# One program for the state-space and the feed-forward stage: first chunk's input made ahead, second matrix's first piece split in four

## The chip, the cores and the metric

The kernel runs on one core of one Trainium2 chip. The metric is the device time of one execution in microseconds, as the median of several runs. Engines by the profile's names: PE is TensorE, PEld its weight loads, DVE is VectorE, ACT is ScalarE, POOL is GpSimd, SP is SyncE, whose queue issues nearly all transfers here.

## The reference

Input x is (2, 2048, 512) float32, the condition t is (2, 512). Two layers follow one another; everything is float32.

```python
# layer 0
mod = t @ Wm + bm                                   # six vectors of 512 per batch element
y_mod = ln(x) * (1 + scale_a) + shift_a
y = x + gate_a * s5(y_mod)                          # diagonal complex recurrence, 128 states
y_norm = ln(y) * (1 + scale_c) + shift_c            # scale_c, shift_c from t @ Wc + bc
h = gelu((y_norm * (1 + scale_ff) + shift_ff) @ W1 + b1)   # 512 -> 2048
z = y + gate_ff * (h @ W2 + b2)                     # 2048 -> 512
# layer 1: conditioned layer norm, attention with 16 heads over 2048 positions,
# projection, second conditioned layer norm, residual
```

## The kernel before

Six stages follow one another: preparation (the condition's vectors, the recurrence's tables), state space, feed-forward, the projection to queries, keys and values, attention, and the last projection. Each is a block of its own with one instruction stream for each engine; engines inside a block meet through semaphores only, and at the end of a block all of them meet at a barrier. Before its end, the state-space block's SP stream also waits for all its loads and for the stores of y (L461).

Every float32 product is made of three matmuls (L36 to L38): an operand is split into a rounded high part and the rest, `hi` and `lo`.

**Preparation** loads Wm (512 x 3072) by three transfers of 2 MB into one tile `wm` (L144); PE's first group of projections waits for the first two of them, the second group for the third and for Wc. ACT copies the projections out, POOL adds the biases (L171), and DVE builds the tables and then the vectors (L366 to L386).

**State space** goes in eight steps c over chunks of 512 positions (c % 2 is the batch element). For each: DVE takes moments of the chunk (`moments`, L578), ACT normalises it into `norm` (L530), PE transposes it (`turn`, L472), ACT applies gain and shift and makes `u` and `u_hi` (`modulate`, L538, L541), POOL makes `u_lo` (L677), PE multiplies into the states (`project_in`), DVE and POOL rotate, scan and rotate back (L641, L664, L645, L650, L672), ACT makes `s_hi` (L548), POOL makes `s_lo` (L682), PE multiplies back (`project_out`, four parts t of 128 positions), and DVE adds the rows (L604). The order of an engine is written out by hand, with chunk c + 1 prepared beside chunk c. SP loads and stores the chunks, and loads three of the four column pieces of W1 (the first two and the last) and, at the last step, `y_first`, the stored first chunk of the result.

**Feed-forward** goes through the same eight chunks. W1 is four pieces (1, 0) to (1, 3), W2 four pieces (2, 0) to (2, 3), each 128 x 2048 values, all kept in `hi` and `lo` parts. For chunk 0 the moments and the normalisation (DVE, L55 to L81, L964), the transposes (PE, L835), gain and shift (ACT, L905) and the split (DVE, L971, L973) come first, among them the split of the first weights: ACT makes the high part of (1, 0), (1, 1), (1, 3), (2, 0) (L893), DVE the low part of (1, 0), (1, 1), (2, 0) (L770), POOL the rest (L1029, L770):

```python
    HI_ACT = [(1, 0), (1, 1), (1, 3), (2, 0)]
    LO_DVE = [(1, 0), (1, 1), (2, 0)]
    POOL = [(1, 3), (2, 1), (1, 2), (2, 2), (2, 3)]
    HELD = [[(1, 0), (2, 0), (1, 2), (2, 2), (2, 3)], [(1, 1), (2, 1)], [(1, 3)]]
    LOADS = [(2, 0), (2, 1), (1, 2), (2, 2), (2, 3)]
```

`HELD` names the three staging tiles (`raw_weight` and two `w_stage`) and what each holds in turn; a load into a tile waits until the piece in it is split. Then each chunk goes through 16 steps j: `up(j)` (12 matmuls into h), ACT's gelu (L911) and high part `h_hi` (L918), DVE's low part `h_lo` (L983), and `down(j)` (12 matmuls into four accumulators). PE's order is up(0), up(1), down(0), up(2), down(1), and so on. up(j) needs piece (1, j // 4), down(j) needs piece (2, j // 4) and h_lo(j). Of chunk 0, PE reads a piece for the first time at up(0), down(0), up(4), down(4), up(8), down(8), up(12), down(12). POOL adds `lift` to the chunk's rows (L1019) and, at the end of a chunk, the result (L1023).

Of the kernel before, what the change touches and what calls it, by code (L numbers as in the profile page):

```python
# [88 lines left out]
def prep_stage(nc, sb, sem, psum, a, ident, columns, s5, x, wgb, vec_dram):  # L89


    wm = sb("wm", [P, KT, 6 * D])
# [38 lines left out]
    with nc.Block() as block:  # L131
        @block.sync
        def _(sp):
# [8 lines left out]
            for n in range(3):  # L142
                cols = slice(2 * n * D, 2 * (n + 1) * D)
                sp.dma_start(wm[:, :, cols], a["L0_cond_Wm"].rearrange("(k p) n -> p k n", p=P)[:, :, cols]).then_inc(ld_wm[n], 16)  # L144
# [29 lines left out]
        def _(pe):  # L174
# [15 lines left out]
            for group, first in enumerate(range(0, 10, SIDE)):  # L190
                if group == 0:
                    pe.wait_ge(ld_wm[0], 16)
                    pe.wait_ge(ld_wm[1], 16)
                if group == 1:
                    pe.wait_ge(bbar_ready, 1)
                    for part in range(2):
                        for k in range(KT):
                            mm = pe.transpose(psum[:, 2 + part, k * P:(k + 1) * P], b_bar[:, part, k * P:(k + 1) * P], ident[:, :])
                        mm.then_inc(bc_tp, 1)
                    pe.wait_ge(ld_wm[2], 16)  # L200
                    pe.wait_ge(ld_wc, 16)
# [14 lines left out]
                for k in range(KT):  # L216
                    for n in range(first, min(first + SIDE, 10)):
                        w = wm[:, k, n * D:(n + 1) * D] if n < 6 else (
                            wc[:, k, (n - 6) * D:(n - 5) * D] if n < 8 else wm[:, k, (n - 8) * D:(n - 7) * D])
# [11 lines left out]
        def _(act):  # L231
# [19 lines left out]
            for j in range(2 * KT):  # L251
                act.wait_ge(gb_tp, j + 1)
                act.activation(wm[:, j % KT, j // KT * D:(j // KT + 1) * D], psum[:, j % 4, :], ACT.Copy).then_inc(gb_ready, 1)
# [135 lines left out]
def s5_stage(nc, sb, sem, psum, a, ident, columns, s5, x, w1_stage, y_first, vec_dram, y_dram):  # L389
# [4 lines left out]
    y = [sb(f"y{b}", [P, TT, D]) for b in range(B)]  # L394
    norm = sb("norm", [P, TT, D])
# [7 lines left out]
    u_hi, u_lo = ([sb(f"u_{part}{n}", [P, KT, CH], F32R) for n in range(NU)] for part in ("hi", "lo"))  # L403
# [5 lines left out]
    x_ld, y_ld, y_st = ([sem(f"s5_{n}{b}") for b in range(B)] for n in ("x_ld", "y_ld", "y_st"))  # L409
    gate_ld, w1_ld, y_first_ld, start = sem("s5_gate_ld"), sem("s5_w1_ld"), sem("s5_y_first_ld"), sem("s5_start")  # L410
# [9 lines left out]

    def rows(dram, c):
# [4 lines left out]
    with nc.Block() as block:  # L426
        @block.sync
        def _(sp):
            def load_x(c):
                sp.wait_ge(norm_ready, TT * (c - 1))  # L430
                sp.dma_start(x[c % B][:, :, :], rows(a["x"], c)).then_inc(x_ld[c % B], 16)

            def load_y(c):
                if c >= B:
                    sp.wait_ge(y_st[c % B], 16 * (c // B))
                sp.dma_start(y[c % B][:, :, :], rows(a["x"], c)).then_inc(y_ld[c % B], 16)

            def store(c):
                sp.wait_ge(y_ready, TT * (c + 1))
                sp.dma_start(rows(y_dram, c), y[c % B][:, :, :]).then_inc(y_st[c % B], 16)  # L440

            for b in range(B):
                sp.dma_start(gate[b][:, :], vec_dram[V_GATE_A, b:b + 1, :].broadcast_to((P, D))).then_inc(gate_ld, 16)
            load_x(2)
            load_y(0)
            for tile, piece in zip(w1_stage, (0, 1, 3)):
                sp.dma_start(tile[:, :, :], a["L0_cond_W1"].rearrange("(k p) f -> p k f", p=P)[:, :, piece * D:(piece + 1) * D]).then_inc(w1_ld, 16)
            for c in range(STEPS):
                if c + 3 < STEPS:
                    load_x(c + 3)  # L450
                if c > 0:
                    load_y(c)
                if c == STEPS - 1:
                    sp.dma_start(y_first[:, :, :], rows(y_dram, 0)).then_inc(y_first_ld, 16)
                if c > 0:
                    store(c - 1)
            store(STEPS - 1)
            sp.wait_ge(w1_ld, 48)
            sp.wait_ge(y_first_ld, 16)
            for b in range(B):  # L460
                sp.wait_ge(y_st[b], 16 * NCH)  # L461

        @block.tensor
        def _(pe):
            def turn(c, ks):

                pe.wait_ge(norm_ready, TT * (c + 1))
                for k in ks:
                    if KT * c + k >= 2:
                        pe.wait_ge(u_ready, 2 * (KT * c + k - 1))  # L470
                    for t in range(TT):
                        mm = pe.transpose(psum[:, TR + k % 2, t * P:(t + 1) * P], norm[:, t, k * P:(k + 1) * P], ident[:, :])  # L472
                    mm.then_inc(tr_ready, 1)

            def project_in(c):

                if c >= B:
                    pe.wait_ge(back_ready, 4 * (c - 1))
                for k in range(KT):
                    pe.wait_ge(ulo_ready, KT * c + k + 1)  # L480
                    for n in range(2):
# [38 lines left out]
        def _(act):  # L520
# [38 lines left out]
            for c in range(STEPS):  # L559
                if c + 2 < STEPS:  # L560
                    take_root(c + 2)
                if c + 1 < STEPS:
                    modulate(c + 1)
# [1548 lines left out]
```

## Time and profile before

| | us |
|---|---|
| median of 3 runs | 3102.53 (3099.68 to 3111.16) |
| the profiled execution | 3103.81 |
| its span, from the first to the last instruction | 3102.0 |
| PE busy in the span | 2956.4 (95%) |
| mean granted TensorE clock | 0.977 |

An instruction belongs to a line of the kernel. "Idle before" is how long its engine had nothing to do ahead of it, and the releaser is what ended that. Names in a row are those of the tiles without their numbers (`w_hi` for both matrices' high parts, `w_stage` for the two staging tiles, which also carry g and a chunk of y in the feed-forward stage).

### The profile page before, as it was taken

What the parts mean: (1) busy time and instruction counts of PE and PEld (TensorE: products, weight loads), DVE (VectorE), ACT (ScalarE), POOL (GpSimd) and SP (SyncE); (2) the same over time, 40 slices, a digit from 0 to 9 for tenths busy, and PEclk for the clock granted to TensorE, in tenths of its full rate; (3) what the DMA queues carried; (4) which work ended last, traced back from release to release, by engine and by line L of the source; (5) the groups of instructions that cost most, each with busy time, mean ns of one, the idle gap of its engine ahead of it and who ended that gap; (6) DMA issues with size and microseconds to landing.
All of it is one profiled execution on the core that took longest, in us unless ns stands there. A gap on an engine that the chain in (4) does not pass through costs nothing. (4 is left out here: it accounts for less than half of the span.)

```text
span 3102.0 us, 41235 instructions
## 1 busy us (share of the span) xinstructions
PE 2956.4 (95%) x15050; PEld 1937.7 (62%) x15050; DVE 2013.7 (65%) x3567; ACT 1509.9 (49%) x2743; POOL 1741.9 (56%) x742
## 2 busy tenths in 40 slices
PE   4897999999999799999999999999999999999987
PEld 2786878878887687765555555555555555555456
DVE  7864332222221555778888888888888888888448
ACT  3532233232332222146666666666666666666634
POOL 2763210111110211138888888888889888888834
PEclk7998999999999899999999999999999999999989
DMA  5433100000000446375668866687765877666557
GB/s 220 154 136 122 41 22 7 28 28 27 28 14 4 166 181 216 132 186 118 133 129 186 185 133 136 130 185 158 153 137 128 172 163 163 135 132 129 109 198 276
DMA packets 148124, 395.73 MB, mean 128 GB/s; under 512 B 11430, under 2 KB 29354, under 8 KB 127448
## 3 DMA queue, kind: packets, MB, share of 16 engines
q0 software_dynamic: 22608, 164.64, 26.5%
q1 hardware_dynamic: 125322, 228.50, 23.7%
q8 instruction: 122, 2.00, 0.3%
q14 instruction: 72, 0.59, 0.1%
HBM read 144.25 MB, written 83.92 MB: 74 GB/s over the span
## 5 line engine op out<-in xcount | busy, mean ns | idle before, releaser
L1679 ACT ACTIVATE probs<-psum 128x512 f32<-128x512 f32 x2048 | 1053.2, 612 | 551.2 <-PE psum L1597 548.5
L1705 DVE TENSOR_REDUCE part_max<-psum 128x1 f32<-128x512 f32 x1984 | 1219.0, 681 | 123.0 <-PE psum L1582 120.4
L1812 POOL TENSOR_TENSOR pair<-probs 128x2048 f32<-128x2048 f32 x255 | 1194.2, 4714 | 150.5 <-ACT probs L1679 144.9
L1597 PE MATMUL psum<-queries,keys 97*128 97x512 f32 x2048 | 849.7, 417 | 5.2 <-ACT probs L1679 2.8
L1582 PE MATMUL psum<-keys,queries 96*128 96x512 f32 x1984 | 802.5, 405 | 2.8
L1597 PEld LDWEIGHTS psum<-queries,keys 97*128 97x128 f32 x2048 | 386.5, 189 | 341.2 <-issue 210.9
L1609 PE MATMUL psum<-probs,values 128*32 128x512 f32 x4096 | 494.0, 600 | 0.0
L1582 PEld LDWEIGHTS psum<-keys,queries 96*128 96x128 f32 x1984 | 376.8, 190 | 125.5 <-DVE part_max L1705 48.4
L983 DVE TENSOR_TENSOR h_lo<-w_stage,h_hi 128x512 fp32r<-128x512 f32 x128 | 99.5, 777 | 515.8 <-ACT h_hi L918 515.8
L911 ACT ACTIVATE w_stage<-psum,b_col 128x512 f32<-128x512 f32 x128 | 88.1, 689 | 498.2 <-PE psum L38 498.2
L1609 PEld LDWEIGHTS psum<-probs,values 128*32 128x32 f32 x4096 | 107.0, 109 | 234.4 <-ACT probs L1679 136.1
L36 PE MATMUL psum<-ffn_u_hi,w_hi 128*128 128x512 f32 x512 | 203.0, 396 | 3.2 <-DVE b_col L1000 3.1
L36 PE MATMUL psum<-w_hi,h_hi 128*128 128x512 f32 x512 | 204.2, 399 | 1.0 <-DVE h_lo L983 1.0
L37 PE MATMUL psum<-w_hi,h_lo 128*128 128x512 f32 x512 | 202.9, 396 | 0.0
L38 PE MATMUL psum<-ffn_u_lo,w_hi 128*128 128x512 f32 x512 | 202.6, 396 | 0.0
L37 PE MATMUL psum<-ffn_u_hi,w_lo 128*128 128x512 f32 x512 | 202.5, 395 | 0.0
L38 PE MATMUL psum<-w_lo,h_hi 128*128 128x512 f32 x512 | 202.2, 395 | 0.0
L1023 POOL TENSOR_TENSOR w_stage<-w_stage 128x512 f32<-128x512 f32 x16 | 20.1, 1284 | 320.1 <-DVE w_stage L989 320.1
L1795 POOL DMA_DIRECT2D pair<-pair x157 | 136.1, 867 | 105.6 <-issue 51.5
L1023 POOL TENSOR_TENSOR y_first<-w_stage,y_first 128x512 f32<-128x512 f32 x16 | 20.2, 1292 | 287.1 <-DVE w_stage L989 287.1
L1268 ACT ACTIVATE qk_hi<-psum,bqkv_col 128x512 fp32r<-128x512 f32 x64 | 44.0, 687 | 213.0 <-PE psum L38 206.6
L1729 DVE TENSOR_TENSOR summed<-psum,summed 128x512 f32<-128x512 f32 x65 | 45.0, 692 | 125.4 <-PE psum L1629 125.4
(312 smaller groups left out, 3733.6 us busy)
## 6 DMA issues: line engine op xcount, KB each, us to landing
pair<-pair POOLq DMA_DIRECT2D x157, 1024.0 KB, 7.3
queries<-q_parts SPq DMA_DIRECT2D x96, 256.0 KB, 5.2
keys<-k_parts SPq DMA_DIRECT2D x42, 512.0 KB, 8.9
x<-in_x_dram SPq DMA_DIRECT2D x8, 1024.0 KB, 7.8
y<-in_x_dram SPq DMA_DIRECT2D x8, 1024.0 KB, 6.1
y_rows<-y SPq DMA_DIRECT2D x8, 1024.0 KB, 4.4
qkv_z<-z_rows SPq DMA_DIRECT2D x8, 1024.0 KB, 5.6
q_parts<-qk_hi SPq DMA_DIRECT2D x32, 256.0 KB, 2.0
```

What stands on the lines that cost most here:

```text
L36: nc.tensor.matmul(out, w_hi, x_hi, start=first, stop=False)
L37: nc.tensor.matmul(out, w_lo, x_hi, start=False, stop=False)
L38: return nc.tensor.matmul(out, w_hi, x_lo, start=False, stop=last)
L911: act.activation(g[j % 2], psum[:, H + j % 2, :], ACT.Gelu_apprx_tanh, bias=b1_col[:, j:j + 1]).then_inc(g_ready, 1)
L983: dve.tensor_tensor(h_lo[j % NH][:, :], g[j % 2], h_hi[j % NH][:, :].bitcast(F32), ALU.subtract).then_inc(glo_ready, 1)
L1582: nc.tensor.matmul(ring_slot(), queries[count % NQ][0:R, h, qt * P:(qt + 1) * P], keys[b][0:R, h, kc * CH:(kc + 1) * CH], start=True, stop ...
L1597: nc.tensor.matmul(psum[:, SC + unit % 3, :], keys[place(count)[0]][0:R + 1, h, kt * P:(kt + 1) * P], queries[count % NQ][0:R + 1, h, :], ...
L1609: mm = nc.tensor.matmul(psum[h * HD:(h + 1) * HD, OUT, :], values[b][:, kt, h * HD:(h + 1) * HD], probs[tile % NPROB][:, h, :], start=(kt ...
L1679: act.activation(probs[tile % NPROB][:, h, :], psum[:, SC + unit % 3, :], ACT.Exp).then_inc(exp_ready, 1)
L1705: dve.tensor_reduce(part_max[:, h * TT + qt, kc:kc + 1], max_slot(), AX.X, ALU.max).then_inc(max_read, 1)
L1795: pool.dma_start(pair[number % NPAIR][:, :, :], pair[(number - 1) % NPAIR][:, :, :], accum_op=ALU.add).then_inc(folded[n % 2], 16)
L1812: pool.tensor_tensor(pair[number % NPAIR][:, :, :], probs[2 * number % NPROB][:, :, :], probs[(2 * number + 1) % NPROB][:, :, :], ALU.add) ...
```

## The change

The two stages become one block: each engine runs its state-space stream and then its feed-forward stream, with no barrier between. What follows is moved with it.

- The feed-forward input of chunk 0 is made by the state-space stage as a ninth chunk, c = 8, beside steps 6 and 7: moments and inverse on DVE, normalisation and modulation on ACT, transposes on PE, the low part on POOL. `y_first` is loaded at step 3 instead of step 7, and b1's rows are loaded at the start.
- (1, 0) is split in the state-space stage: ACT makes the high part after step 6, DVE the low part at the start of step 7. SP then loads (2, 0) into its place at step 7.
- The feed-forward streams of ACT, DVE, POOL and SP begin with `finished`, which waits until the last rows are added; PE's begins with a wait for the ninth chunk's u_lo. Counters that chunk 0 would have raised are raised by hand.
- (2, 0) is split in four parts of 512 columns, ACT and DVE following each other. All six other pieces go to POOL, in the order in which PE needs them, after DVE's last part. The product of b2 and the gate (`lift`) moves from DVE to POOL.
- W1 and W2 parts become tiles of one piece each. Some tiles are lent to the preparation, for which Wm is loaded in six transfers of 1 MB instead of three of 2 MB.

```diff
 # preparation
-            for n in range(3):
-                cols = slice(2 * n * D, 2 * (n + 1) * D)
-                sp.dma_start(wm[:, :, cols], ...[:, :, cols]).then_inc(ld_wm[n], 16)
+            for n in range(6):
+                sp.dma_start(wm[n][:, :, :], ...[:, :, n * D:(n + 1) * D]).then_inc(ld_wm[n // 2], 16)
 # state space, SP
+        sp.dma_start(ahead["b1_rows"][:, :], ...).then_inc(small_ld, 16)
-            for tile, piece in zip(w1_stage, (0, 1, 3)):
+        for piece, tile in enumerate(w1_stage[:2]):
...
-                if c == STEPS - 1:
+            if c == B + 1:
                 sp.dma_start(y_first[:, :, :], rows(y_dram, 0)).then_inc(y_first_ld, 16)
+            if c == STEPS - 1:
+                sp.wait_ge(wlo_dve, 1)
+                sp.dma_start(w1_stage[0][:, :, :], ...W2 piece 0...).then_inc(w_ld[0], 16)
             if c > 0:
                 store(c - 1)
         store(STEPS - 1)
-            sp.wait_ge(w1_ld, 48)
-            sp.wait_ge(y_first_ld, 16)
-            for b in range(B):
-                sp.wait_ge(y_st[b], 16 * NCH)
 # PE: turn(c + 1, ...) without "if c + 1 < STEPS"; ACT: take_root, normalise up to c + 2 <= STEPS
             modulate(c + 1)
...
             split_state(c)
+            if c == STEPS - 2:
+                act.wait_ge(norm_ready, TT * STEPS)
+                act.wait_ge(w1_ld, 32)
+                act.activation(ahead["w1_hi"][:, :, :], w1_stage[0][:, :, :], ACT.Copy).then_inc(whi_ready, 1)
 # DVE
-                if c + 2 < STEPS:
+            if c + 2 <= STEPS:
                 moments(c + 2)
                 invert(c + 2)
+            else:
+                dve.wait_ge(whi_ready, 1)
+                dve.tensor_tensor(ahead["w1_lo"][:, :, :], w1_stage[0][:, :, :], ahead["w1_hi"][:, :, :].bitcast(F32), ALU.subtract).then_inc(wlo_dve, 1)
+    def finished(engine):
+        engine.wait_ge(cy_ready, TT * STEPS)
+        engine.wait_ge(y_ready, TT * STEPS)
+        engine.wait_ge(shi_ready, 2 * STEPS)
+        engine.wait_ge(slo_ready, 2 * STEPS)
+    def first_input(engine):
+        engine.wait_ge(ulo_ready, KT * (STEPS + 1))
 # feed-forward
+    HI_ACT = [(1, 0), (2, 0)]
+    LO_DVE = [(1, 0), (2, 0)]
+    POOL = [(1, 1), (1, 2), (2, 1), (2, 2), (1, 3), (2, 3)]
+    HELD = [[(1, 0), (2, 0), (1, 2), (2, 2), (1, 3), (2, 3)], [(1, 1), (2, 1)]]
+    LOADS = [(1, 2), (2, 1), (2, 2), (1, 3), (2, 3)]
...
 # ACT, after finished and six sem_inc
+            for f in range(FP):
+                act.activation(w2_hi[p][:, f, :], raw(w, p)[:, f, :], ACT.Copy).then_inc(whi_ready, 1)
 # DVE, after finished, six sem_inc and the copy of b1_col
+            for f in range(FP):
+                dve.wait_ge(whi_ready, 1 + f + 1)
+                dve.tensor_tensor(w2_lo[p][:, f, :], raw(w, p)[:, f, :], w2_hi[p][:, f, :].bitcast(F32), ALU.subtract).then_inc(wlo_dve, 1)
 # POOL
+        state_space["finished"](pool)
+        pool.wait_ge(wlo_dve, 1 + FP)
+        for n, (w, p) in enumerate(POOL):
+            wait_loaded(pool, w, p)
+            if w == 2 and p >= NP - B:
+                state_space["stored"](pool, p - (NP - B))
+            pool.tensor_copy(part(w1_hi, w2_hi, w, p), raw(w, p)).then_inc(whi_pool, 1)
+            pool.wait_ge(whi_pool, n + 1)
+            split_low(pool, w, p, wlo_pool)
 # one block
+                def _(pe):
+                    one["tensor"](pe)
+                    two["tensor"](pe)
```

## Rows read from the trace of the kernel before

**Rows 1.** The page: PE's busy tenths, the span in 40 slices of 77.55 us.

```profile
PE   4897999999999799999999999999999999999987
```

**Rows 2.** Windows: us, busy us (count) by engine, granted clock, DMA share, GB/s.

```profile
13.00:15.00 2.00, 0.00 (x0) 0.00 (x0) 1.71 (x9) 0.00 (x0) 0.00 (x0) 1.00 1.02 420
82.00:84.00 2.00, 0.00 (x0) 0.00 (x0) 2.00 (x4) 0.00 (x0) 0.00 (x0) 0.98 1.04 384
...
155.60:174.60 19.00, 18.54 (x114) 16.18 (x113) 14.94 (x29) 9.75 (x15) 14.41 (x11) 1.00 0.49 167
191.70:210.60 18.90, 18.43 (x114) 16.10 (x114) 11.24 (x14) 7.44 (x11) 14.35 (x11) 1.00 0.31 112
244.50:272.50 28.00, 9.12 (x31) 7.04 (x32) 21.49 (x33) 12.17 (x11) 4.71 (x1) 0.63 0.45 131
```

**Rows 3.** Timeline of PE across the boundary: start, us, engine, line, [idle before].

```profile
243.20 0.27 PE L38 MATMUL psum<-s_d_lo,u_hi 128*128 128x128 f32 x1
...
267.60 0.49 PE L36 MATMUL psum<-ffn_u_hi,w_hi 128*128 128x512 f32 x1 [3.09 <-DVE b_col L1000]
274.83 0.39 PE L36 MATMUL psum<-w_hi,h_hi 128*128 128x512 f32 x1
280.42 0.39 PE L36 MATMUL psum<-w_hi,h_hi 128*128 128x512 f32 x1
```

**Rows 4.** Timeline of DVE and ACT: boundary, split of constants, preparation.

```profile
206.51 0.77 ACT L541 ACTIVATE u_hi<-psum,columns 128x512 fp32r<-128x512 f32 x1
243.51 0.69 DVE L604 TENSOR_TENSOR y<-psum,y 128x512 f32<-128x512 f32 x1 [2.05 <-PE psum L38]
249.37 1.91 ACT L893 ACTIVATE w_hi<-raw_weight 128x2048 fp32r<-128x2048 f32 x1 [21.54 <-PEq L426]
260.42 2.28 DVE L770 TENSOR_TENSOR w_lo<-raw_weight,w_hi 128x2048 fp32r<-128x2048 f32 x1
75.58 2.18 ACT L557 ACTIVATE s_c_hi<-prod 128x512 fp32r<-128x512 f32 x4
79.94 2.49 DVE L624 TENSOR_TENSOR s_c_lo<-prod,s_c_hi 128x512 fp32r<-128x512 f32 x4
269.84 1.28 ACT L911 ACT_TABLE_LOAD   x1
31.68 1.29 DVE L356 TENSOR_TENSOR s_b_lo<-psum,s_b_hi 128x512 fp32r<-128x512 f32 x2 [5.35 <-ACT s_b_hi L248]
```

**Rows 5.** Timeline of PE and POOL in steps 6 and 7 of the state space.

```profile
226.41 0.50 PE L36 MATMUL psum<-s_c_hi,s_hi 128*128 128x512 f32 x1 [1.36 <-DVE y L604]
230.87 0.73 PE L36 MATMUL psum<-s_c_hi,s_hi 128*128 128x512 f32 x1
...
198.88 2.52 POOL L664 TENSOR_TENSOR turned<-prod 128x512 f32<-128x512 f32 x2 [4.22 <-DVE prod L641]
211.03 2.54 POOL L682 TENSOR_TENSOR s_lo<-state,s_hi 128x512 fp32r<-128x512 f32 x2
217.84 2.53 POOL L664 TENSOR_TENSOR turned<-prod 128x512 f32<-128x512 f32 x2 [4.27 <-DVE prod L641]
```

**Rows 6.** Timeline of ACT, DVE and POOL in chunk 0 of the feed-forward stage.

```profile
272.24 0.69 ACT L911 ACTIVATE w_stage<-psum,b_col 128x512 f32<-128x512 f32 x1 [1.12 <-PE psum L38]
273.71 0.69 DVE L983 TENSOR_TENSOR h_lo<-w_stage,h_hi 128x512 fp32r<-128x512 f32 x1 [0.37 <-ACT h_hi L918]
310.08 2.84 DVE L983 TENSOR_TENSOR h_lo<-w_stage,h_hi 128x512 fp32r<-128x512 f32 x1 [4.92 <-ACT h_hi L918]
305.77 1.90 POOL L1029 CAST w_hi<-raw_weight 128x2048 fp32r<-128x2048 f32 x1 [5.36 <-DMA raw_weight<-in_L_cond_W_dram]
307.75 4.62 POOL L770 TENSOR_TENSOR w_lo<-raw_weight,w_hi 128x2048 fp32r<-128x2048 f32 x1
```

**Rows 7.** DMA issues from 0 to 345 us: KB each, median us to landing.

```profile
raw_weight<-in_L_cond_W_dram SPq DMA_DIRECT2D x5, 1024.0 KB, 5.2
w_stage<-in_L_cond_W_dram SPq DMA_DIRECT2D x3, 1024.0 KB, 12.8
```

More of the change, by code:

```diff
@@ L402, in s5_stage @@
     u = [sb(f"u{n}", [P, CH]) for n in range(2)]
-    u_hi, u_lo = ([sb(f"u_{part}{n}", [P, KT, CH], F32R) for n in range(NU)] for part in ("hi", "lo"))
+    u_hi, u_lo = ([sb(f"u_{part}{n}", [P, KT, CH], F32R) for n in range(NU - 1)] + [ahead[f"u_{part}"]] for part in ("hi", "lo"))
     prod = sb("prod", [P, 4, CH])
@@ L419, in s5_stage, with chunk_in @@
     TR, BU, CY = 0, 2, 6
+    def chunk_in(c):
+        return x[c % B] if c < STEPS else y_first
     def rows(dram, c):
@@ L701, in ffn_stage @@
+def ffn_stage(nc, sb, sem, psum, a, ident, columns, state_space, ahead, stage, y_first, vec_dram, y_dram, z_dram):
+    NP = 4
+    FP = FT // NP
+    w1_hi, w1_lo = ([ahead[f"w1_{n}"]] + [sb(f"w1_{n}{p}", [P, KT, FP * P], F32R) for p in range(1, NP)] for n in ("hi", "lo"))
+    w2_hi = [sb(f"w2_hi{p}", [P, FP, D], F32R) for p in range(NP - B)] + ahead["w2_hi"]
+    w2_lo = [sb(f"w2_lo{p}", [P, FP, D], F32R) for p in range(NP)]
     y = [y_first, stage[1]]
-    norm = sb("ffn_norm", [P, TT, D])
+    norm = ahead["norm"]
@@ L2054, in cond_seq_kernel @@
         with ExitStack() as weights:
-            w1_stage = [raw_weight] + [scope(weights)(f"w1_stage{n}", [P, KT, D]) for n in (1, 2)]
-            y_first = scope(weights)("y_first", [P, TT, D])
+            keep = scope(weights)
+            w1_stage = [raw_weight] + [keep(f"w1_stage{n}", [P, KT, D]) for n in (1, 2)]
+            y_first = keep("y_first", [P, TT, D])
+            with ExitStack() as early:
+                plain = scope(early)
+                x = [plain(f"s5_x{n}", [P, TT, D]) for n in range(B)]
+                lent = [plain(f"lent{n}", [P, KT, D]) for n in range(2)]
+                y = [plain(f"s5_y{n}", [P, TT, D]) for n in range(B)]
+            ahead = {f"w1_{part}": keep(f"w1_{part}0", [P, KT, D], F32R) for part in ("hi", "lo")}
+            ahead.update({f"u_{part}": keep(f"u_{part}_first", [P, KT, CH], F32R) for part in ("hi", "lo")})
+            ahead["w2_hi"] = [keep(f"w2_hi_late{b}", [P, KT, D], F32R) for b in range(B)]
+            ahead["norm"], ahead["b1_rows"] = keep("norm", [P, TT, D]), keep("b1_rows", [FT, P])
+            ahead["y"] = y
+            lent = [tile[:, :, :] for tile in y + [ahead["norm"]] + lent]
             with ExitStack() as state_space:
```

951 lines of the change are left out of this document (471 added, 480 removed).

## The prediction

> **What bounds the kernel now.** I read the page first. PE is at nine tenths in nearly every slice; the first two, the fourth, the fourteenth and the last two are lower [rows 1]. The fourth slice is the boundary that the change touches, so I went to the windows, then to each engine's timeline across it. The window of 28 us there has PE busy for 9.12 us at a granted clock of 0.63 [rows 2]. PE's timeline shows the hole: its last state-space matmul starts at 243.20 (ends 243.47), its first feed-forward matmul at 267.60, and `down(0)` at 274.83, 5.59 us before `down(1)` [rows 3]. Between them lie the last row addition (ends 244.20), the store and the barrier up to 249.37 [rows 4], then chunk 0's moments, normalisation, transposes and split. From `down(0)` on PE runs step after step of 5.59 us (2.80 for an `up`, 2.80 for a `down`). So the price of the change is how much earlier `down(0)` comes, and whether what PE needs later still comes in time. All times below are in the time of before; a shift of the preparation is added at the end.
>
> **Change part by part.**
>
> *Wm in six transfers.* PE's first projections wait for 4.19 MB of Wm, and DVE idles 5.35 us behind them before s_b_lo [rows 4], so this is on the path of the preparation. The present transfers run at 420 GB/s; transfers with rows of 2 KB (the chunks of x, the pieces of W1) ran at 384 [rows 2]. 4.19 MB take 10.0 us at 420 and 10.9 at 384. Bounds 0 and 0.9 us; I take 0.7 later, near the upper end, since the row length is like that of the 384. Three more issues on SP come ahead of transfers that are needed later.
>
> *The ninth chunk on DVE and ACT in step 6: nothing.* The window from 155.60, one step long, holds the same work for an earlier chunk: 19.00 us with DVE busy 14.94. Step 6, without it, takes 18.90 with DVE at 11.24 [rows 2]. The 3.7 us are covered by PE's 18.4 busy us. Then the split of (1, 0): ACT's modulation ends at 207.3, the normalisation and s_hi are six copies of that kind, about 4 us, w1_hi takes 1.91 and w1_lo on DVE 2.28 [rows 4]: it ends near 215.5. DVE has nothing else then until step 7's products, which start about 1.3 us before POOL's 217.84 [rows 5]. If that cover were gone, step 7's products would be late by the excess. y_first is loaded four steps early; its SP issue costs 0.5 us ahead of a store that waits anyway.
>
> *PE in step 7.* The ninth chunk adds 16 transposes, 2.1 us at full clock. PE idles now because DVE's additions come late (1.36 us before 226.41) [rows 5], and they fit in there. But POOL now makes two u_lo before s_lo. In step 6, which has them, s_lo starts 211.03 - 198.88 = 12.15 us after the first `turned` [rows 5]. Step 7's `turned` starts at 217.84, so s_lo starts at 229.99 and its halves are done at about 231.3 and 232.5, while PE is free at 229.3. `project_out(7)` therefore begins 2.0 us later than PE could, with a second stop of 0.55, where it now begins at 230.87 [rows 5]. On the other side, the part from 226.41 took 4.46 us [rows 5] where the last ones, at full clock, come every 0.69 + 2.05 = 2.74 [rows 4]: after PE's idle time the granted clock was at its lower level, 1.2 GHz. If it stays at 2.4 GHz the state space ends 0.7 us earlier than now, if it falls as long as before 2.5 later. I take no change: last matmul ends 243.5, last addition 244.2.
>
> *The boundary.* Barrier and store go (the stores drain behind POOL's late pieces); b1's transpose is one matmul. Each engine waits and raises six counters: between 0.2 us (one releaser, as from PE to DVE) and 1.0; the whole boundary of before, from the last addition to ACT's first copy, took 5.2 us with all of it. I take 0.4: `up(0)` and ACT's first part of (2, 0) start at 244.6. Now the order from there. PE: `up(0)` to 247.4, `up(1)` to 250.2. ACT: four 128x512 copies take 2.18 us [rows 4], to 246.8; the table load 1.28 [rows 4], to 248.1; then gelu and h_hi to h_lo's start 1.47 (272.24 to 273.71) [rows 6], so h_lo(0) starts at 249.6 and ends at 250.3. `down(0)` starts at 250.4, instead of 274.83: **24.4 us earlier**. DVE's four parts take 2.49 [rows 4] behind ACT's first, so they end at 247.8, and `down(0)` does not wait for them.
>
> *POOL's six pieces.* A piece takes 1.90 + 0.08 for the cast and 4.62 for the low part [rows 6]; I use 6.9 (the longest low part of before was 5.04). A load lands after 5.2 us at the median [rows 7]. POOL starts at 247.9. (1,1) is done at 254.8, needed by `up(4)` at 264.4. (1,2), loaded from 247.8, is done at 261.7, needed at 286.8. (2,1), loaded from 254.8, is done at 268.6, needed by `down(4)` at 250.4 + 4 x 5.59 = 272.8. (2,2) 275.5 for 295.1; (1,3), whose load waits for (2,2), 275.5 + 5.2 + 6.9 = 287.6 for 309.1; (2,3) 299.7 for 317.5. The smallest slack is 4.2 us. `lift` (1.3 on DVE) and L1019 come after and end before 310, where they began at 312.
>
> *POOL against DVE.* The row that matters is h_lo at 310.08: 2.84 us long instead of 0.69, and it ends at 312.92, 0.55 after POOL's low part ends at 312.37 [rows 6]. So h_lo waits out a POOL subtraction that is under way. From its start to the `down` that needs it there are 5.6 - 1.65 = 3.95 us, so a collision costs PE something only if h_lo comes within 1.3 us of the start of a 4.65 us low part, at most 1.3 us each. There are six now, where only POOL's five were. By the order above, the low part of (1,2) starts at 257.3 and h_lo(2) comes at 257.7: about 0.9 lost. Bounds 0 and 3 us; I take 1.0.
> The Trainium skill has the rule (SBUF — State Buffer, "Who interferes with whom"): a VectorE instruction with two SBUF inputs and a GpSimd instruction that reads SBUF exclude each other for a whole instruction, and the one that issues first wins. The trace agrees, with the 2.84 us. By it a collision is decided by hundredths of a microsecond, which is the first rival.
>
> **The sum.** 24.4 earlier, less 0.7 (Wm), less 1.0 (collisions): 22.7. The profiled execution took 3103.81 (1.8 around its span), which gives 3081.1; it stood 1.3 above the median of the runs. On the median: 3102.5 - 22.7 = **3080**. Later stages are the same instructions.
>
> **Rivals.**
>
> *1. POOL's first low part gets ahead of h_lo(0).* POOL's cast starts at 247.9, so its first low part wants to start at 249.8; h_lo(0) wants 249.6. The margin is 0.2 us, made of terms that I know to 0.1 each. If POOL is first, h_lo(0) ends 0.55 after it: 249.8 + 4.7 + 0.55 = 255.0, and `down(0)` at 255.1, 4.7 us later; with PE idle for that long the clock may fall, as after 226.41 [rows 5], another 0 to 2 us. Gain 16 to 18: **3085 to 3087**. For it: the thin margin; against: ACT, at 246.8, has a head start on DVE.
>
> *2. PE's clock is low in the first `up`s.* PE is idle for 1.1 to 1.5 us after the last state-space matmul. Before, 1.36 us of idle time was followed by 1.7 us lost in the next part [rows 5], but no fall came at once after 243.47. If it falls, or if the state-space tail ends 2.5 later, `up(0)` takes up to 5.6, h_lo(0) falls behind POOL's low part and rival 1 comes too. Gain 13 to 15: **3087.5 to 3089.5**.
>
> *3. The other side: loads of the pieces come late.* (1,2), (2,2), (1,3) and (2,3) pass through one tile, each load waiting for the split before it, so the last is ready at 247.6 + 4 (L + 7) with a landing time L. Needed at 317.5, it costs nothing up to L = 10.5. The three loads into `w_stage` had a median of 12.8 [rows 7], under the traffic of step 0: then 326.8, **3089**, no real change against rival 1. It ends slower than 3118 only when it costs 38 us, from L = 20. For it: stores and y loads share the queue. Against: the loads into `raw_weight`, at this very place, 5.2.
>
> *4. The parts hide nothing.* If chunk 8's work delayed steps 6 and 7 by all it adds (3.7 on DVE, 4.2 for the weights, 2.1 on PE), 10 us of the gain would go: 3090. The window of a full step speaks against it [rows 2].
>
> **How the numbers follow.** My forecast 0.52, with 3076 to 3084 as its own range (Wm 0 to 0.9, collisions 0 to 3, tail -0.7 to +0.7, wake-up 0.2 to 1.0). Rival 1: 0.23. Rival 2: 0.10. Rivals 3 and 4 with some gain left: 0.09; slower: 0.03. Better than 3075: 0.03. The range of 3075 to 3088 leaves out the 0.03 below, half of rival 2, and rivals 3 and 4: 0.2. A difference of 0.5%, 15.5 us, is about what a measurement of this kernel can tell from no change, so the border is 3087.0: faster 0.52 + 0.03 + 0.22 + 0.02 = 0.79, within it 0.18, slower 0.03.
>
> **What would show it.** Right: PE's gap between its last state-space and first feed-forward matmul is about 1.2 us instead of 24.1, `down(0)` 7 us after it; PE's wait before `project_out(7)` is about 2 us, for POOL's s_lo; steps 2 to 6 stay near 18.95; POOL's pieces end near 300. Rival 1: h_lo(0) is over 4 us long. Rival 2: the granted clock is half in the window of `up(0)`. Wm: the last vector L386 comes 0.7 later. Wrong would be a wait of PE for a POOL piece, or step 7 starting late behind w1_lo.

## The result and the profile after

The kernel after runs in 3078.85 us (median of 4 runs, 3076.78 to 3080.23), the kernel before in 3102.2 beside it: ratio 0.9919, 95% interval 0.9898 to 0.994. The profiled execution took 3080.23 with a span of 3078.4, against 3102.0 before: 23.6 us less.

The page of after, PE's busy tenths in 40 slices of 76.96 us, answers to [rows 1]: the fourth slice is full now.

```profile
PE   4899999999998999999999999999999999999987
```

The timeline of PE in after, from the last step of the state space to the last `down` (start, duration, [idle before <- what ended it]); it answers to [rows 3] and [rows 5].

```profile
227.43 0.50 PE L36 MATMUL psum<-s_c_hi,s_hi 128*128 128x512 f32 x1 [0.48 <-DVE s_y L604]
232.03 0.73 PE L36 MATMUL psum<-s_c_hi,s_hi 128*128 128x512 f32 x1 [1.65 <-POOL s_lo L684]
...
245.93 0.49 PE L36 MATMUL psum<-u_hi_first,w_hi 128*128 128x512 f32 x1 [1.03 <-DVEq L966]
246.26 0.39 PE L37 MATMUL psum<-u_hi_first,w_lo 128*128 128x512 f32 x1
...
251.82 0.49 PE L36 MATMUL psum<-w_hi,h_hi 128*128 128x512 f32 x1
...
313.63 0.51 PE L36 MATMUL psum<-w_hi_late,h_hi 128*128 128x512 f32 x1 [3.55 <-DVE h_lo L1002]
...
345.16 0.40 PE L36 MATMUL psum<-u_hi_first,w_hi 128*128 128x512 f32 x1
...
978.28 0.40 PE L38 MATMUL psum<-w_lo,h_hi 128*128 128x512 f32 x1
```

The same two places in before, `up(0)` of chunk 1 and the last matmul of the stage:

```profile
360.91 0.39 PE L36 MATMUL psum<-ffn_u_hi,w_hi 128*128 128x512 f32 x1
...
1002.42 0.40 PE L38 MATMUL psum<-w_lo,h_hi 128*128 128x512 f32 x1
```

`down(0)` stands at 251.82 instead of 274.83, 23.0 us earlier; the last matmul of the stage stood at 1002.42 before and stands at 978.28, 24.1 earlier. Between these two rows lie two changes that nearly cancel. From `down(0)` to `up(0)` of chunk 1, chunk 0 takes 345.16 - 251.82 = 93.34 us, where before it took 360.91 - 274.83 = 86.08: **7.3 us lost**. From there to the last `down`, 978.28 - 345.16 = 633.12 instead of 1002.42 - 360.91 = 641.51: **8.4 us gained**, in chunks whose instructions the change leaves alone. The stages behind took 0.6 us longer in this execution, so 23.6 are left in the whole.

Where chunk 0 loses them, in the timeline of DVE and POOL in after (answers to [rows 6]):

```profile
250.91 0.78 DVE L1002 TENSOR_TENSOR h_lo<-w_stage,h_hi 128x512 fp32r<-128x512 f32 x1 [1.83 <-ACT h_hi L941]
275.74 4.70 DVE L1002 TENSOR_TENSOR h_lo<-w_stage,h_hi 128x512 fp32r<-128x512 f32 x1 [2.30 <-ACT h_hi L941]
...
299.59 4.61 DVE L1002 TENSOR_TENSOR h_lo<-w_stage,h_hi 128x512 fp32r<-128x512 f32 x1 [3.56 <-ACT h_hi L941]
304.32 1.05 DVE L73 TENSOR_TENSOR ffn_ln_off<-ffn_ln_inv 128x4 f32<-128x4 f32 x1
308.32 4.66 DVE L983 TENSOR_SCALAR norm<-w_stage,ffn_ln_inv,ffn_ln_off 128x512 f32<-128x512 f32 x4
312.90 1.28 DVE L1002 TENSOR_TENSOR h_lo<-w_stage,h_hi 128x512 fp32r<-128x512 f32 x2
...
251.23 4.92 POOL L788 TENSOR_TENSOR w_lo<-w_stage,w_hi 128x2048 fp32r<-128x2048 f32 x1
258.97 1.90 POOL L1044 CAST w_hi<-raw_weight 128x2048 fp32r<-128x2048 f32 x1 [2.83 <-DMA raw_weight<-in_L_cond_W_dram]
303.61 2.98 POOL L1049 TENSOR_TENSOR ffn_lift<-ffn_lift,ffn_gate 128x512 f32<-128x512 f32 x2
306.84 5.40 POOL L1032 TENSOR_TENSOR y_first<-y_first,ffn_lift 128x512 f32<-128x512 f32 x4 [0.26 <-POOL ffn_lift L1049]
```

Two kinds of collision are to be seen. First, seven `h_lo` of chunk 0 wait for an instruction of POOL. Four of them (from 253.18 to 270.20) last 1.8 to 3.5 us and cost PE nothing; three start within 0.8 us of a low part's start and last 4.4 to 4.7 us instead of 0.69. The three steps from one `up` to the next take 6.51, 6.24 and 6.43 us instead of 5.54, together 2.6 lost. Second, and larger: from 303.6 to 312.2 POOL multiplies `lift` and adds it to y (L1049, L1032), and in just this time DVE makes chunk 1's normalisation. A small operation on 4 columns (L73) takes 1.05 instead of 0.16, the four normalisations 4.66 instead of 1.92, and the `h_lo` that stand behind them end at 314.18. PE waits 3.55 for the first of them, up to 313.63, and then runs at 1.2 GHz (granted clock 0.56 from 313.60 to 317.00); that one step takes 10.91, 5.4 lost. In before the same operations of DVE stand free of POOL:

```profile
323.00 0.16 DVE L73 TENSOR_TENSOR ffn_ln_off<-ffn_ln_inv 128x4 f32<-128x4 f32 x1
...
324.08 1.92 DVE L964 TENSOR_SCALAR ffn_norm<-w_stage,ffn_ln_inv,ffn_ln_off 128x512 f32<-128x512 f32 x4
```

There POOL's four additions began at 312.3, behind its last piece, and were over when DVE began to normalise at 322.8.

Where the later chunks gain: matmuls grouped by line and names over full chunks (first fence before, second after; columns: count, busy us, mean ns of one).

```profile
L36 PE MATMUL psum<-ffn_u_hi,w_hi 128*128 128x512 f32 x433 | 171.0, 395 | 0.1
L38 PE MATMUL psum<-w_lo,h_hi 128*128 128x512 f32 x432 | 170.6, 395 | 0.0
```

```profile
L36 PE MATMUL psum<-u_hi_first,w_hi 128*128 128x512 f32 x437 | 170.7, 391 | 0.0
L38 PE MATMUL psum<-w_lo,h_hi 128*128 128x512 f32 x440 | 174.1, 396 | 0.0
```

Only the matmuls with u are shorter. From start to start, the twelve of an `up` take 2.73 us instead of 2.79, those of a `down` 2.81 as before; a step is 5.54 instead of 5.60. These instructions are the same; what differs is where their tiles lie. Over the 112 steps from chunk 1 on this makes 6.4 of the 8.4 us.

The other 2 us are of another kind, read off the rows and not tried by an edit of its own. At a chunk's start POOL adds `lift` to y while DVE makes the chunk's first `h_lo`, and which of the two starts first differs from build to build. In before POOL was first at chunks 2 and 4 (here chunk 2), and the steps there took 0.7 and 0.8 us more, with further parts of a microsecond in the steps beside them:

```profile
457.39 1.65 DVE L983 TENSOR_TENSOR h_lo<-w_stage,h_hi 128x512 fp32r<-128x512 f32 x1 [1.85 <-ACT h_hi L918]
457.19 5.93 POOL L1019 TENSOR_TENSOR y_first<-y_first,ffn_lift 128x512 f32<-128x512 f32 x4
459.17 0.49 PE L36 MATMUL psum<-w_hi,h_hi 128*128 128x512 f32 x1 [0.50 <-DVE h_lo L983]
```

In after, at the same place, DVE was first by 0.17 us:

```profile
440.39 0.75 DVE L1002 TENSOR_TENSOR h_lo<-w_stage,h_hi 128x512 fp32r<-128x512 f32 x1 [1.50 <-ACT h_hi L941]
440.56 5.96 POOL L1032 TENSOR_TENSOR y_first<-y_first,ffn_lift 128x512 f32<-128x512 f32 x4
```

Two builds below with the tiles of after, W2's piece whole and POOL released first, have these long steps again and take 635.6 us from chunk 1 on, where after takes 633.1.

### The profile page after: what moved, and what is told of

Its sections match the earlier page's. It is cut to its first block and busy times, and to the rows that moved or that the text cites. A ratio compares the mean times of both kernels' runs of the same rounds, so it can differ in the third digit from the quotient of the medians.

```text
span 3078.4 us, 41263 instructions
## 1 busy us (share of the span) xinstructions
PE 2943.5 (96%) x15050; PEld 1935.5 (63%) x15050; DVE 2014.2 (65%) x3553; ACT 1511.7 (49%) x2752; POOL 1760.6 (57%) x751
## 5 line engine op out<-in xcount | busy, mean ns | idle before, releaser
L1002 DVE TENSOR_TENSOR h_lo<-w_stage,h_hi 128x512 fp32r<-128x512 f32 x128 | 112.2, 877 | 500.9 <-ACT h_hi L941 500.9
L36 PE MATMUL psum<-u_hi_first,w_hi 128*128 128x512 f32 x512 | 200.1, 391 | 1.0 <-DVEq L966 1.0
L37 PE MATMUL psum<-u_hi_first,w_lo 128*128 128x512 f32 x512 | 199.7, 390 | 0.0
L38 PE MATMUL psum<-u_lo_first,w_hi 128*128 128x512 f32 x512 | 199.5, 390 | 0.0
L38 PEld LDWEIGHTS psum<-w_lo,h_hi 128*128 128x128 f32 x512 | 97.0, 189 | 23.9
L36 PEld LDWEIGHTS psum<-u_hi_first,w_hi 128*128 128x128 f32 x512 | 96.2, 188 | 23.0 <-ACTq L908 1.1
```

The source lines that it names most:

```text
L36: nc.tensor.matmul(out, w_hi, x_hi, start=first, stop=False)
L37: nc.tensor.matmul(out, w_lo, x_hi, start=False, stop=False)
L38: return nc.tensor.matmul(out, w_hi, x_lo, start=False, stop=last)
L1002: dve.tensor_tensor(h_lo[j % NH][:, :], g[j % 2], h_hi[j % NH][:, :].bitcast(F32), ALU.subtract).then_inc(glo_ready, 1)
```

## Experiments on the later chunks' gain: where u lies

The kernel before ran beside each group of kernels on its chip, at 3103.5, 3105.0, 3106.5 and 3105.7 us; so whole times are compared by their ratio to it, and small effects within the profiled executions.

The places below are added up from the shapes in the kernel. Tiles lie one behind another, each rounded up to 32 bytes per partition. A tile of [128, 4, 512] has 8192 bytes per partition, a multiple of 256, so the byte of a 256-byte group at which tiles start is moved only by the small ones. The tiles of W1 and W2 start at byte 224 in both kernels. Before, u stands behind them, a statistics tile of 96 and six of 32 bytes: 224 + 288 = 512, byte 0. After, u has moved among the large tiles, to byte 224. The h tiles are at byte 64 in both.

**Pads before and after.** A pad of 32 bytes ahead of u, first in the kernel before (it moves h too), then in the kernel after (there u goes to byte 0, a second pad behind it moves W1's later pieces and W2 to 32).

```diff
 # before
+    sb("pad_u", [P, 8])
     u_hi = sb("ffn_u_hi", [P, KT, CH], F32R)
 # after
+                plain("pad_e", [P, 16])   # among the tiles lent before
+            keep("pad_u0", [P, 8])
             ahead.update({f"u_{part}": keep(f"u_{part}_first", [P, KT, CH], F32R) for part in ("hi", "lo")})
+            keep("pad_u1", [P, 8])
```

> The kernel before with one unused tile of 32 bytes for each partition ahead of the feed-forward u_hi, so that u_hi and u_lo start 32 bytes later (181280 instead of 181248; the weight tiles start at an odd multiple of 32). In the changed kernel an up takes about 2.73 us instead of 2.80, though its matmuls are the same; a down is unchanged. Theory P (placement: the 12 matmuls of an up are faster when u and the weights start on the same residue of 64 bytes): up takes 2.73 here too, the pitch of a step j falls from 5.59 to 5.54, the kernel gains 8 to 10 us with nothing else of the change in it. Theory W (the weights as tiles of one piece each, with rows of 2 KB instead of 8, make it) and theory L (u lies lower in the memory, at 49888): no change, within 2 us.

> The changed kernel with 32 bytes ahead of u_hi_first and 32 behind u_lo_first (and 64 in the tiles lent before, so that nothing else changes its residue of 64). Theory P: up goes back to 2.80, the pitch of a step from 5.54 to 5.59, and the kernel is 7 to 9 us slower than the changed one: about 3087, against the kernel before only 0.5% faster. Theories W and L: 3079, as the changed kernel.

Measured: the kernel before with the pad 3100.21 us (ratio to before 0.9985, interval 0.9975 to 0.9994), an `up` 2.76; the kernel after with the pads 3087.39 (0.9947, 0.993 to 0.9964), an `up` back at 2.79 and the last `down` at 986.14 instead of 978.28. So the gain of after hangs on u's place: one pad takes back 7.9 us, about 0.9 of them by a long first step of chunk 2 as described above. W1's first piece did not move in that run and its `up`s are as long as the others, so W1's place alone is not it. In the kernel before, the pad gave a third of what theory P (placement) asked; the theory was incomplete.

**96 and 224 bytes in the kernel before.** With a pad of 96, then of 224 bytes ahead of u, and of 32 behind it so that h keeps its byte of 128 or 256.

```diff
+    sb("pad_u0", [P, 24])   # the other run: [P, 56]
     u_hi = sb("ffn_u_hi", [P, KT, CH], F32R)
     u_lo = sb("ffn_u_lo", [P, KT, CH], F32R)
+    sb("pad_u1", [P, 8])
     b1_rows = sb("b1_rows", [FT, P])
```

> The kernel before, with one unused tile of 96 bytes per partition ahead of its two feed-forward u tiles and one of 32 bytes behind them, so that the u tiles start at byte 96 of a 128-byte group, as the tiles of W1 that they are multiplied with do, and the h tiles stay where they were within their groups. Theory P (the place of u relative to the other operand, counted in groups of 128 bytes, sets the length of an up): with 32 bytes the step fell from 5.60 to 5.56 only; here it should be 5.54, an up 2.72 instead of 2.79, the last gate of the feed-forward stage some 8 us earlier (before: 1000.75), the whole near 3094 to 3095. Rival Q (only the page of 64 bytes or the mere shift counts): 5.56 and 3098 to 3100 again. Rival N (chance): 5.60 and no change.

> The kernel before, with an unused tile of 224 bytes per partition ahead of its u tiles and one of 32 behind them, so that the u tiles start at byte 224 of a 256-byte group, as the tiles of W1 do (in the kernel after u starts at 224 of 256 as well; the kernel before has 0 there, the run with 32 bytes 32, the run with 96 bytes 96); the h tiles stay where they were within their groups of 256. Theory P2 (what counts is that both operands start at the same byte of a group of 256): an up falls from 2.79 to 2.73, the step from 5.60 to 5.54, the last gate of the feed-forward stage comes near 993 instead of 1000.75, the whole near 3095 to 3097. Rival Q2 (the kernel after owes its shorter up to the layout of W1 in four pieces of its own, and to u's place together): an up stays at 2.77 to 2.79, the whole at 3099 to 3103.

Measured: 96 bytes, an `up` at 2.79 and 3101.25 us (0.9988, 0.9978 to 0.9998): groups of 128 are refuted. 224 bytes, an `up` at 2.73 as in after, 3098.93 us (0.9975, 0.9965 to 0.9985). The `up` came out as expected, the whole less so: from chunk 1's `up(0)` on the stage took 635.5 us instead of 641.5, so 6.0 of the 8.4 us come with u's place alone, in a run that kept the two long steps of chunks 2 and 4. But chunk 0 was 3.8 longer than in before, in its first steps, where `h_lo` wait for POOL for over 4 us several times; in before the longest there lasts 2.84 us. From `down(0)` to chunk 1 the four builds of the kernel before take 86.1 to 87.7 us, so one or two of the 7.3 us lost in chunk 0 hang on how the collisions happened to fall in before.

**The h tiles.** If the byte of 256 counts, `down` can be shortened too: its operands, h at byte 64 and W2 at 224, don't match.

```diff
+    sb("pad_h", [P, 40])
     h_hi = [sb(f"h_hi{n}", [P, CH], F32R) for n in range(NH)]
```

> The kernel after, with an unused tile of 160 bytes per partition ahead of its four h tiles, so that they start at byte 224 of a 256-byte group (64 before), as the tiles of W2 that they are multiplied with do. Theory P2 (the same byte of a group of 256 for both operands shortens a matmul, whichever of them is the weight): a down falls from 2.81 to about 2.73, the step from 5.54 to 5.47, the last gate of the feed-forward stage 8 to 10 us earlier than 976.67, the whole 3069 to 3072. Rival (only the moving operand's place counts, which for a down is W2 and stays at 224): a down stays at 2.80 to 2.81 and the whole at 3078 to 3080.

Measured: 3069.46 us (0.9872, 0.9855 to 0.9888), the step 5.44, the last `down` at 968.36. In the lines by name of this run:

```profile
L38 PE MATMUL psum<-w_lo,h_hi 128*128 128x512 f32 x439 | 170.9, 389 | 0.0
L36 PE MATMUL psum<-u_hi_first,w_hi 128*128 128x512 f32 x437 | 170.1, 389 | 0.0
```

The `down` matmul fell from 396 to 389 ns, start to start the twelve from 2.81 to 2.72; here the tile that was moved is the stationary operand, in an `up` it is the moving one. The `up` fell a little more, from 2.73 to 2.72.

**Everything by 32 bytes.** In the kernel with h moved, all four at byte 0 instead of 224.

```diff
+            keep("pad_all", [P, 8])
             w1_stage = [raw_weight] + [keep(f"w1_stage{n}", [P, KT, D]) for n in (1, 2)]
```

> The run with the h tiles at byte 224 of 256 (3069.46), with one unused tile of 32 bytes per partition at the front, so that every tile behind it (both operands of every up and down: u, W1, h, W2) moves by 32 bytes, from byte 224 to byte 0 of a group of 256. Theory E (what counts is that both operands start at the same byte of the group): the step stays at 5.44 to 5.45, the last down ends near 968.4, the whole within 3 us of 3069. Rival F (byte 224 itself is what is fast): the step goes back to 5.54 to 5.60, the last down comes 10 to 18 us later, the whole 3079 to 3087.

Measured: 3073.55 us (0.9896, 0.9881 to 0.9911), the step 5.44, 721.8 us from the first `up` to the last `down`, where the run with h alone moved had 722.0. Byte 224 itself is not what is fast; equal bytes are, in the two places tried. (The profiled execution took 3068.71; the median of the others is a few us higher, and the profile doesn't say where.) The bytes and lengths together:

| run | u | W1 | `up` us | h | W2 | `down` us |
|---|---|---|---|---|---|---|
| before | 0 | 224 | 2.79 | 64 | 224 | 2.81 |
| 32 bytes, before | 32 | 224 | 2.76 | 96 | 224 | 2.80 |
| 96 bytes, before | 96 | 224 | 2.79 | 192 | 224 | 2.80 |
| 224 bytes, before | 224 | 224 | 2.73 | 64 | 224 | 2.81 |
| after | 224 | 224 | 2.73 | 64 | 224 | 2.81 |
| pads, after | 0 | 224, 32 | 2.79 | 128 | 32 | 2.81 |
| h moved, after | 224 | 224 | 2.72 | 224 | 224 | 2.72 |
| all moved | 0 | 0 | 2.72 | 0 | 0 | 2.72 |

The table counts in groups of 256 bytes, but groups of 512 fit all eight rows as well. Groups of 1024 don't: in the run with 224 bytes u stands 512 bytes off W1 and its `up` is short.

## Experiments on the boundary and chunk 0

**Normalisation later.** The moments of the next chunk at step 11 instead of 8, its normalisation at 13 instead of 10.

```diff
-    LN_TILE = 8
+    LN_TILE = 11
```

> The changed kernel with LN_TILE = 11 instead of 8: the next chunk's moments and inverse come at steps 11 and 13 instead of 8 and 10. In the changed kernel chunk 0 is 8 us longer than 16 undisturbed steps; PE waits 3.6 us for h_lo(10), which is queued on DVE behind the normalisation, which waits for POOL's subtraction, the product for lift and the additions to y_first. Theory C (POOL and DVE keep each other out, and the normalisation at step 10 falls on POOL's last piece): the wait of 3.6 goes and with it the low clock behind it, 4 to 5.5 us faster than the changed kernel, about 3074. Rival D (PE waits for POOL's pieces or for a single h_lo, not for the normalisation): no more than 1 us.

Measured: the step of 10.91 us is gone, and from the first `up` to the last `down` the stage takes 974.26 - 246.04 = 728.2 us instead of 732.4 (978.28 - 245.93). In chunk 0 itself 5.3 us come back (88.01 instead of 93.34 from `down(0)` to chunk 1), and the normalisation, now behind POOL's additions, takes 1.92 for the four again; the later chunks are 1.2 longer, most of it a long first step of chunk 2. So the second kind of collision is shown to cost about 5 us. The whole kernel did not follow: 3079.99 us (0.9925, 0.9909 to 0.9942), because the stages behind took about 4 us longer in the profiled execution; they contain no edit. Over all builds the time behind the last `down` lies between 2098.2 and 2104.5 us, so differences of a few us in the whole say nothing of a change in one stage.

**GpSimd's order in the last step.** `s_lo` of step 7 ahead of the last two `u_lo` of the ninth chunk.

```diff
-            split(c + 1, (2, 3))
+            if c < STEPS - 1:
+                split(c + 1, (2, 3))
             split_state(c)
+            if c == STEPS - 1:
+                split(c + 1, (2, 3))
...
         # in `finished`
+        engine.wait_ge(ulo_ready, KT * (STEPS + 1))
```

> The kernel after, with POOL's order in the last state-space step turned round: s_lo(7) first, then the last two u_lo of the ninth chunk. Theory (PE stops 1.65 us for s_lo and then runs 3 us at the lower clock because POOL makes two u_lo first): both go, the last state-space matmul and down(0) come 2.5 to 3.3 us earlier (down(0) at 248.5 to 249.3 instead of 251.8), the whole 3075.5 to 3076.5. Rival (PE is then late for another operand, the products of DVE or y): PE's wait moves and the gain is under 1 us. Rival (u_lo of the ninth chunk comes late for up(0) or pushes POOL's pieces): up(0) gets a wait for u_lo and the gain at down(0) is smaller than at the last state-space matmul.

Measured: 3078.61 us (0.9911, 0.9894 to 0.9927). The timeline of PE in this run:

```profile
226.98 0.51 PE L36 MATMUL psum<-s_c_hi,s_hi 128*128 128x512 f32 x1 [0.47 <-DVE s_y L604]
...
229.78 0.45 PE L36 MATMUL psum<-s_c_hi,s_hi 128*128 128x512 f32 x1
...
242.10 0.49 PE L36 MATMUL psum<-u_hi_first,w_hi 128*128 128x512 f32 x1 [1.02 <-DVEq L970]
```

The stop before `project_out(7)` is gone, its first matmul takes 0.45 instead of 0.73, and from the part at 226.98 to the first `up` it is 15.12 us, where after has 245.93 - 227.43 = 18.50: 3.4 us, where the theory had 2.5 to 3.3. Part of it is the clock: two builds with the old order (normalisation later, and POOL released first) kept 2.4 GHz behind the same stop and have 17.4, so against them the new order gives 2.3. The whole missed the expected 3075.5 to 3076.5 and can't be told from after; the stages behind took 2.9 us longer.

**The first piece of W2 whole again.** One copy on ACT and one subtraction on DVE.

```diff
-            for f in range(FP):
-                act.activation(w2_hi[p][:, f, :], raw(w, p)[:, f, :], ACT.Copy).then_inc(whi_ready, 1)
+            act.activation(w2_hi[p][:, :, :], raw(w, p), ACT.Copy).then_inc(whi_ready, 1)
 # DVE, likewise: one subtraction behind it; PE and POOL wait for that one
```

> The kernel after, with the first piece of W2 split whole again (one ACT copy, one DVE subtraction behind it) instead of in four parts. Theory (the four parts take the split off the path: DVE finishes 0.6 us behind ACT instead of a whole subtraction of 2.3): DVE's subtraction ends near 250.5 instead of 249.1, POOL's first low part starts 1.4 later and so is clearly behind h_lo(0); down(0) within 0.3 us of 251.8, the whole 3078 to 3080: the parts are worth nothing by themselves. Rival (h_lo(0), which DVE makes after the subtraction, or POOL's cast, which then falls on it, comes late): down(0) 1 us or more later than 251.8.

3081.55 us, one run, which can't be told from after. In the timelines of DVE and POOL:

```profile
246.11 2.29 DVE L1012 TENSOR_TENSOR w_lo<-raw_weight,w_hi 128x2048 fp32r<-128x2048 f32 x1 [1.63 <-ACT w_hi L915]
248.87 2.14 DVE L1001 TENSOR_TENSOR h_lo<-w_stage,h_hi 128x512 fp32r<-128x512 f32 x1 [0.47 <-ACT h_hi L940]
...
248.57 1.89 POOL L1042 CAST w_hi<-w_stage 128x2048 fp32r<-128x2048 f32 x1 [17.13 <-DVE w_lo L1012]
```

My theory fell and the rival's mechanism holds: `h_lo(0)` meets POOL's cast, lasts 2.14 and ends 0.55 behind it. From the first `up` to `down(0)` it is 6.97 us instead of 5.89: the parts are worth 1.1 us there. (`down(0)` itself stands at 251.14, because this build's first `up` came 1.8 us earlier than that of after; so only the distance between the two can be compared.)

**GpSimd's start.** Released after DVE's third part, then after its first, instead of the fourth.

```diff
         state_space["finished"](pool)
-        pool.wait_ge(wlo_dve, 1 + FP)
+        pool.wait_ge(wlo_dve, FP)      # the other run: 1 + 1
```

> The changed kernel with POOL released after the third of DVE's four parts of (2, 0) instead of the fourth, so that its cast of (1, 1) starts about 0.6 us earlier and its first subtraction would start at 250.6, ahead of h_lo(0) at 250.9. Theory R (rival 1 of the prediction: whoever starts first keeps the other out for the whole instruction): h_lo(0) takes 4 to 5.3 us instead of 0.78 and ends 0.55 after the subtraction, down(0) starts near 256 instead of 251.8, and the kernel loses 4 to 6 us. Rival: the two share, h_lo(0) takes under 1.5 us and nothing is lost. If DVE's fourth part holds POOL's cast back by 0.5 us, the order stays as it is and the test says nothing.

> The kernel after, with GpSimd released for its pieces after the first of DVE's four parts instead of after all four. Theory (rival 1 of the prediction: POOL's low part gets ahead of h_lo(0), which then waits it out): h_lo(0) over 3 us long, down(0) 3 to 5 us later than 251.8, PE idle before it and at the lower clock after, the whole 3 to 6 us longer than after in the same place. Rival (DVE's parts hold POOL's cast back, so that the order stays): POOL's low part starts within 0.5 us of where it did (251.2) and down(0) does not move.

Released after the third part (3079.42 us, one run), POOL's low part started at 250.16 and `h_lo(0)` at 250.15: the margin of the first rival had shrunk to 0.01 us and DVE was still first. So POOL did not get ahead, and this run says nothing on the price. Released after the first (3084.16 us, one run):

```profile
244.05 8.60 DVE L1014 TENSOR_TENSOR w_lo<-raw_weight,w_hi 128x512 fp32r<-128x512 f32 x4 [0.34 <-ACT w_hi L916]
252.57 1.28 DVE L1002 TENSOR_TENSOR h_lo<-w_stage,h_hi 128x512 fp32r<-128x512 f32 x2
...
244.91 2.19 POOL L1044 CAST w_hi<-w_stage 128x2048 fp32r<-128x2048 f32 x1 [13.25 <-DVE w_lo L1014]
247.17 4.93 POOL L788 TENSOR_TENSOR w_lo<-w_stage,w_hi 128x2048 fp32r<-128x2048 f32 x1
```

```profile
253.38 0.50 PE L36 MATMUL psum<-w_hi,h_hi 128*128 128x512 f32 x1 [2.63 <-DVE h_lo L1002]
253.72 0.50 PE L37 MATMUL psum<-w_hi,h_lo 128*128 128x512 f32 x1
254.02 0.63 PE L38 MATMUL psum<-w_lo,h_hi 128*128 128x512 f32 x1
```

POOL is first, and it is DVE's last part that waits it out (8.60 us for the four instead of 2.50, ending 0.55 after the low part), with `h_lo(0)` behind it. From the first `up` to `down(0)`: 253.38 - 243.40 = 9.98 instead of 5.89, 4.1 us; PE idles 2.63 and its matmuls then last 0.63, at 1.2 GHz (granted clock 0.50 from 254.00 to 257.00). That is the first rival's price (4.7 us, and up to 2 for the clock), paid through another instruction. `down(0)` itself came 1.6 us later than in after, where the expectation had 3 to 5, because the first `up` was 2.5 earlier in this build. The Trainium skill's rule (SBUF — State Buffer, "Who interferes with whom": who issues first has the shared port pair for a whole instruction) agrees with both runs, the 0.01 us and the 8.60.

**The three gains together.** `LN_TILE = 11`, `s_lo` first, h moved by 160 bytes.

> The three edits that gained something, together on the kernel after: s_lo(7) ahead of the ninth chunk's last two u_lo on POOL (last down 3.8 us earlier alone), the next chunk's moments and normalisation at steps 11 and 13 of a chunk instead of 8 and 10 (4.0 earlier alone), and the h tiles at byte 224 of 256 (9.9 earlier alone). Theory (they lie in different places and add up): the last state-space matmul 3.8 earlier, the step 5.44, the last down near 978.3 - 3.8 - 4.0 - 9.9 = 960.6, the whole 3061 to 3065 if the stages behind keep their length. Rival (the collisions of chunk 0 fall differently and give back part): the last down at 962 to 966. Rival (the stages behind take 3 to 4 us longer, as with the norm moved alone): the whole 3065 to 3068.

Measured: **3063.3 us**, ratio 0.9852 (0.9838 to 0.9865), against 0.9919 for after. The last `down` is at 960.54, as the theory has it (960.6). The way there differs a little: the first `up` came at 244.41, since one step near the start of the state space took 22.0 us (20.4 and 18.9 in other builds, this row of after 18.9), and the stage then took 716.1 us where the sum of the parts gives 717.9.

## Why the prediction was right, and where only its total was

**The boundary: right, 0.7 us late.** The gap between PE's last state-space and first feed-forward matmul is about 1.2 us (b1's transpose lies in it). From the first `up` to `down(0)` 5.89, where I had 5.8. `down(0)` came at 251.82 where the working had 250.4, plus 0.7 for Wm: 251.1. Nearly all of the 0.7 left is the state-space tail, which I had taken as no change.

**Wm in six transfers: right as far as it can be told.** The last vector came 0.76 later. Over all profiled executions it stands at 55.4 on the mean with three transfers (4 builds, 54.58 to 56.58) and at 56.1 with six (10 builds, 55.31 to 57.34). A difference of 0.7 with a spread of 2 is no proof of the cause; Wm alone wasn't tried.

**Step 6 and the weights hidden: right.** The part at 227.43 came 1.0 later than before's at 226.41, 0.8 of it from the preparation.

**Step 7: the mechanism right.** PE waited 1.65 for POOL's `s_lo` where I had 2.0, and its clock was at 1.2 GHz behind it: the first matmul takes 0.73, and the granted clock was 0.50 from 232.10 to 235.00. Its last matmul ended at 244.74 instead of 243.47; with 0.7 of that from the preparation the tail took +0.6, of the bounds -0.7 and +2.5. Turning POOL's order round gives back 3.4, about 1.1 of it clock that two of the eight builds with the old order did not lose.

**POOL's pieces: right.** The last ends at 303.65 (I had 299.7), and no piece held PE up. The loads landed in time (waits of POOL 2.83, 5.20, 5.37).

**Collisions: mis-sized, 7 to 8 us where I took 1.0 (bounds 0 and 3).** The term was "a collision costs PE something only if h_lo comes within 1.3 us of the start of a 4.65 us low part", and "about 0.9 lost" for one of them. That sentence holds: the three that came so cost 0.7 to 1.0 each. Two things were missing. I placed only one of the six beside an `h_lo`, and with a slip: by the working's own terms the low part of (1, 2) starts at 254.8 + 1.98 = 256.8, not 257.3, and the loss is 0.3, not 0.9. In the run that low part started at 260.95, and `h_lo(2)`, at 259.12, met the cast before it and cost nothing; the three that cost were other ones. And I let `lift` and L1019 "come after and end before 310" without asking what DVE does in that time: it is chunk 1's normalisation, and that costs 5.4 alone.

**"Later stages are the same instructions": the step that failed.** They are, but their tiles had moved, and the same matmuls became 4 ns shorter: 6.4 us from chunk 1 on and about 0.9 in chunk 0. The code of after has it, in `u_{part}_first` among the tiles made ahead; no row of before would have given me the price. Another 2 us came because two collisions of before, at chunks 2 and 4, did not fall so in after.

So the total is this close (22.7 forecast, 23.6 found) by luck: the collisions cost 7 us more than I had, and 9 us came that the sum had at nothing, 7 by where tiles lie and 2 by chance. The mechanism of the 24 us at the boundary is right on its own. Rival 1 was not taken, by 0.32 us (`h_lo(0)` at 250.91, POOL's low part at 251.23), and costs 4.1 when it is. Rival 2 did not come: the granted clock was 1.00 from 246.30 to 251.00, 2.4 GHz. Nor did rivals 3 and 4.

## What to carry to other kernels

Before calling a stage unchanged, compare where its tiles start, not only its instructions: a pad of 160 bytes was worth 10 us here, more than each edit to the order. When an engine's work is moved earlier, write down what the other engine on its port does at the new time for every instruction moved, the small ones at the end included. When a forecast comes out right, check its terms one by one; here the sum hid two wrong ones. And compare several builds before a gain of 1 or 2 us is put down to an edit: which of two engines starts first can change with hundredths of a microsecond.

## What the runs showed of the hardware

- A matmul of 128x512 fp32 takes some 1 to 3% longer when its stationary and its moving tile start at different bytes of a 256-byte group (2.76 to 2.81 us for twelve against 2.72 to 2.73); groups of 512 bytes fit these runs as well. Both operands' places count, and equal bytes were as fast at 0 as at 224. Not every difference costs the same: 64 bytes apart (u at 32, W1 at 224) cost least. Which mechanism it is, and whether it holds in the attention stages, wasn't tried.
- DVE's waits for POOL also catch operations on 4 columns (1.05 us instead of 0.16) and the normalisation, which reads one tile and two columns (4.66 instead of 1.92 for four).
- Eight builds have the same stop of PE before `project_out(7)`, of 1.63 to 1.66 us. In six it was followed by matmuls of 0.63 us or more, at 1.2 GHz (0.50 granted in after); in the run with POOL released first (1.63) and the one with the normalisation later (1.64) it was not, and the granted clock of the former was 1.00 from 229.00 to 233.00. Idle time alone doesn't foretell it.
